# Expert weights addressed by two plain table numbers instead of one packed code

## What is computed

```python
qkv = rms_norm(x) @ w_qkv.T;  q, k, v = split(qkv)        # the mixer, on layernorm(x)
q, k = rms_norm(q), rms_norm(k)
w  = cumsum(exp(k), axis=1);  kv = cumsum(exp(k) * v, axis=1)
y  = sigmoid(q) * kv / (w + 1e-6)
u, g = split(y @ w_swiglu.T)
x = x + (layernorm(x) + (u * silu(g)) @ w_out.T)

flat = layernorm(x)                                        # the experts, 8 of them, 2 per token
topk = top_k(softmax(flat @ router_weight.T + router_bias), 2)
y = einsum('th,ehk->tek', flat, weight) + bias
x = x + flat + y[topk].sum(over the two)
```

## Time and profile before

| | |
|---|---|
| median of 3 runs | 1638.11 us (1636.93 to 1638.89) |
| the profiled execution, its own time | 1636.89 us |
| its span, first to last instruction | 1635.1 us |
| busy: PE, DVE, ACT, POOL | 1572.5, 1214.4, 570.6, 993.6 us |
| granted TensorE clock, mean | 0.993 |

### The profile page before, as it was taken

The page is one execution under the profiler, slowest core; times in us unless marked ns, Lnnn a source line. Parts: engine busy times, 40 slices in busy tenths (PEclk is TensorE's granted clock), DMA queues, the critical chain, the costliest instruction groups (busy, mean ns, idle before and its releaser), DMA issues.

```text
span 1635.1 us, 27374 instructions
## 1 busy us (share of the span) xinstructions
PE 1572.5 (96%) x7987; PEld 1284.8 (79%) x7987; DVE 1214.4 (74%) x2436; ACT 570.6 (35%) x1088; POOL 993.6 (61%) x1253
## 2 busy tenths in 40 slices
PE   8899999999999999999999999989999867899998
PEld 5788888888888888888888888778788755677786
DVE  7777778877877788778777877897887564565665
ACT  4333333333333333333333333323333222333433
POOL 2546666675577667765766586567663365565663
PEclk9999999999999999999999999999999989999999
DMA  6122333334333343333433343343425587599884
GB/s 234 49 93 91 128 134 126 122 127 147 117 117 117 117 142 127 135 123 132 152 117 117 117 143 116 117 143 117 143 98 188 175 269 227 161 368 372 317 312 178
DMA packets 135387, 258.57 MB, mean 158 GB/s; under 512 B 18519, under 2 KB 19297, under 8 KB 135242
## 3 DMA queue, kind: packets, MB, share of 16 engines
q1 hardware_dynamic: 118442, 222.62, 39.3%
q0 software_dynamic: 16800, 34.21, 6.3%
HBM read 321.00 MB, written 101.11 MB: 258 GB/s over the span
## 4 chain that ended last, share of the span: by engine, by line
PE 87%; DVE 3%; another core or an unknown queue 2%; SPq 2%; issue 2%; DMA 1%; ACT 1%; POOL 0%; POOLq 0%; DVEq 0%; ACTq 0%
PE pU L1348 4%; PE pG L1348 3%; PE pV L1348 3%; PE pG L1350 3%; PE pK L1348 3%; PE pO L1350 3%; PE pO L1348 3%; PE pO L1349 3%; PE pK L1350 3%; PE pG L1349 3%; PE pK L1349 3%; PE pV L1349 3%; PE pV L1350 3%; PE pQ L1348 3%; PE pQ L1349 3%; PE pQ L1350 3%
## 5 line engine op out<-in xcount | busy, mean ns | idle before, releaser
L784 DVE RECIPROCAL B<-B 128x512 f32<-128x512 f32 x64 | 214.6, 3353 | 2.2
L388 POOL TENSOR_SCALAR sa<-ss,hinv,ep 128x1 f32<-128x1 f32 x128 | 44.0, 344 | 238.7 <-ACT B L576 238.2
L402 POOL TENSOR_TENSOR F<-B,F 128x512 fp32r<-128x512 f32 x64 | 82.6, 1290 | 140.5 <-ACT F L598 140.5
L473 POOL DMA_INDIRECT out_dram<-B,tab x91 | 93.8, 1031 | 110.7 <-DVE B L866 66.0
L812 DVE SCALAR_TENSOR_TENSOR B<-B,nm,pO 128x512 f32<-128x512 f32 x64 | 47.8, 746 | 146.5 <-PE pO L1350 146.5
L433 POOL TENSOR_TENSOR R<-B,R 128x512 fp32r<-128x512 f32 x112 | 142.6, 1297 | 0.0
L428 POOL TENSOR_TENSOR B<-B 128x512 f32<-128x512 f32 x112 | 141.8, 1292 | 0.0
L1348 PE MATMUL pK<-R,F 128*128 128x512 f32 x256 | 106.3, 415 | 2.0 <-DVE F L744 2.0
L1348 PE MATMUL pG<-R,F 128*128 128x512 f32 x256 | 106.4, 416 | 1.5 <-POOL F L402 1.4
L1348 PE MATMUL pU<-R,F 128*128 128x512 f32 x256 | 106.3, 415 | 0.0
L1348 PE MATMUL pV<-R,F 128*128 128x512 f32 x256 | 101.4, 396 | 1.5 <-DVE B L758 1.5
(11 more groups left out here) (256 smaller groups left out, 4535.5 us busy)
## 6 DMA issues: line engine op xcount, KB each, us to landing
R<-pair_weights SPq DMA_DIRECT2D x93, 2048.0 KB, 11.7
pair_weights<-R SPq DMA_DIRECT2D x112, 512.0 KB, 3.9
B<-in_wm SPq DMA_DIRECT2D x112, 256.0 KB
B<-pair_biases SPq DMA_DIRECT2D x93, 256.0 KB, 12.4
x_scratch<-B SPq DMA_DIRECT2D x64, 264.0 KB
B<-in_x SPq DMA_DIRECT2D x64, 256.0 KB
B<-in_xt SPq DMA_DIRECT2D x32, 256.0 KB
XTB<-in_xt SPq DMA_DIRECT2D x32, 256.0 KB
```

The source lines that it names most:

```text
L388: p.tensor_scalar(sa[:, r, j:j + 1], ss[:, r, j:j + 1], hinv[:, 0:1], ep[:, r:r + 1], ALU.mult, ALU.add).then_inc(s[f"ra{j}"], 1)
L402: p.tensor_tensor(fr(3)[0], DD, fr(2)[1], ALU.subtract).then_inc(s["yl"], 1)
L473: p.indirect_dma_start(od, bass.IndirectOffsetOnAxis(ap=idx[:, J:J + 1], axis=0), YO[J % 4], None, bounds_check=T * 128 - 1, oob_is_err=Fa ...
L784: v.reciprocal(DD, DD).then_inc(s["rec"], 1)
```

## The change

The table holds plain numbers. `tw` now has slot x 4096, the column at which the slot begins in `R`; the bias block of slot s is now block s of `B`, so that its column is `tw >> 3`. `tc` has the number of the pair, and 64 is added (`SKIP`) where nothing is to be loaded: the address then lies outside of `pair_weights` and `pair_biases`, and the transfer is dropped (`bounds_check="skip_entire_dma"`). The tiles of the mixer that lay in `B`'s blocks 0 to 7 are renumbered, so that each shares its block with the same slot as before. The loads of the numbers no longer state limits (`min_val`, `max_val`).

```diff
+SKIP = 64.0
...
-        X = [blk(0), blk(1), blk(2)]
-        WT, KVT, EQT, DD = blk(4), blk(5), blk(6), blk(7)
-        XT = [blk(3), sb("XTB", [128, 512])[:, :]]
+        X = [blk(6), blk(7), blk(0)]
+        WT, KVT, EQT, DD = blk(2), blk(3), blk(4), blk(5)
+        XT = [blk(1), sb("XTB", [128, 512])[:, :]]
...
             def load_run(r):
                 slot = (6 + r) % 8
-                code = e.value_load(rc[0:1, r:r + 1], min_val=0, max_val=2 * NP - 1)
+                pair = e.value_load(rc[0:1, r:r + 1])
...
             def load_pair(t):
...
-                code = e.value_load(tc[0:1, t:t + 1], min_val=0, max_val=NP * 16 - 1)
-                slot, new, pair = code & 7, (code >> 3) & 1, code >> 4
-                e.dma_start(Rf[:, bass.ds(slot * 4096, 4096)],
+                pair, at = e.value_load(tc[0:1, t:t + 1]), e.value_load(tw[0:1, t:t + 1])
+                e.dma_start(Rf[:, bass.ds(at, 4096)],
                             pwd[bass.ds(pair, 1), :, :].rearrange("o p n -> p (o n)"),
-                            cond=new, max_dma_last_dim=2048).then_inc(dwb[(t - 2) % 8], 16)
+                            bounds_check="skip_entire_dma", max_dma_last_dim=2048).then_inc(dwb[(t - 2) % 8], 16)
...
-                e.dma_start(B[:, bass.ds(((slot + 2) & 7) * 512, 512)], pbd[bass.ds(pair, 1), :].broadcast_to([128, H]),
-                            cond=new).then_inc(dwb[(t - 2) % 8], 16)
+                e.dma_start(B[:, bass.ds(at >> 3, 512)], pbd[bass.ds(pair, 1), :].broadcast_to([128, H]),
+                            bounds_check="skip_entire_dma").then_inc(dwb[(t - 2) % 8], 16)
...
-                return ((v.value_load(tw[0:1, J:J + 1], min_val=0, max_val=7) + 2) & 7) * 512
+                return v.value_load(tw[0:1, J:J + 1]) >> 3
...
-                v.scalar_tensor_tensor(out=q4[:, 1, :], in0=qnum[:, :], scalar=16.0, in1=q4[:, 2, :],
-                                       op0=ALU.mult, op1=ALU.add).then_inc(s["rt"], 1)
+                v.tensor_scalar(q4[:, 2, :], c, 4096.0, None, ALU.mult)
+                v.tensor_scalar(q4[:, 1, :], qnum[:, :], SKIP, None, ALU.add).then_inc(s["rt"], 1)
...
-                at = pe.value_load(tw[0:1, J:J + 1], min_val=0, max_val=7) * 4096
+                at = pe.value_load(tw[0:1, J:J + 1])
```

More of the change, by code:

```diff
@@ L286, in load_run @@
                 slot = (6 + r) % 8
-                code = e.value_load(rc[0:1, r:r + 1], min_val=0, max_val=2 * NP - 1)
+                pair = e.value_load(rc[0:1, r:r + 1])
                 e.dma_start(Rf[:, slot * 4096:(slot + 1) * 4096],
[L289 to L292, removed]
+                            pwd[bass.ds(pair, 1), :, :].rearrange("o p n -> p (o n)"),
+                            bounds_check="skip_entire_dma", max_dma_last_dim=2048).then_inc(drun[r // 2], 16)
+                e.dma_start(blk(slot), pbd[bass.ds(pair, 1), :].broadcast_to([128, H]),
+                            bounds_check="skip_entire_dma").then_inc(drun[r // 2], 16)
             def load_pair(t):
@@ L954, in slots_of @@
                 ready()
-                v.scalar_tensor_tensor(out=q4[:, 2, :], in0=c, scalar=-8.0, in1=runq[:, :],
+                v.scalar_tensor_tensor(out=c, in0=c, scalar=-8.0, in1=runq[:, :],
                                        op0=ALU.mult, op1=ALU.add).then_inc(s["rt"], 1)
@@ L1074, in table @@
                     ready()
-                    v.scalar_tensor_tensor(out=ge, in0=qnum[:, :], scalar=0.5, in1=ge,
+                    v.scalar_tensor_tensor(out=ge, in0=qnum[:, :], scalar=-SKIP, in1=ge,
                                            op0=ALU.add, op1=ALU.mult).then_inc(s["rt"], 1)
@@ L1081, in table @@
                     ready()
-                    v.scalar_tensor_tensor(out=ge, in0=ge, scalar=2.0, in1=c,
-                                           op0=ALU.mult, op1=ALU.mult).then_inc(s["rt"], 1)
+                    v.tensor_tensor(ge, ge, c, ALU.mult).then_inc(s["rt"], 1)
                     yield
@@ L1113, in table @@
                 ready()
-                v.scalar_tensor_tensor(out=col, in0=c4[:, 3:4], scalar=8.0, in1=c4[:, 1:2],
+                v.scalar_tensor_tensor(out=col, in0=c4[:, 3:4], scalar=-SKIP, in1=c4[:, 1:2],
                                        op0=ALU.mult, op1=ALU.add).then_inc(s["rt"], 1)
@@ L1125, in table @@
                     ready()
-                    v.tensor_copy(rc[:, :], pX[0:1, 480:484]).then_inc(s["rt"], 1)
+                    v.tensor_scalar(rc[:, :], pX[0:1, 480:484], SKIP, None, ALU.add).then_inc(s["rt"], 1)
                 yield "table"
```

## The result

| | before | changed |
|---|---|---|
| median of 5 runs | 1638.11 us (1635.35 to 1638.89) | 1728.3 us (1727.57 to 1728.48) |
| span of the profiled execution | 1635.1 us | 1726.6 us |
| granted TensorE clock, mean | 0.993 | 0.992 |

The changed kernel takes 1.0547 times as long [1.0534, 1.0559]: 90 us more, where 72 were forecast, inside the range of 1690 to 1753.

What follows compares the result with a forecast made beforehand. TensorE's own pace, 3.21 us a tile, was taken as the bound, its sequencer running ahead at 1.9 us. A 4.3 us sequencer round adds 61 us in the second part and 11 in the first: 1710 us, range 1690 to 1753.

Steps and rivals of the forecast that it cites:

- TensorE's part, one k: TensorE's sequencer in the expert stage: three matmuls of one k take 415, 98 and 415 ns, 928 where TensorE needs 690.
- low end (151): Four-step test's added step free, 151 ns: 898 ns a k, round 4.2 us, +54, nothing in the first part, 1692 us.
- high end (190): Four-step test costs VectorE's 190 ns: 1036 ns a k, round 4.74 us, +90, with 25 in the first part, 1753 us.
- The round, 4.3 us: TensorE's sequencer needs 4.3 us a tile against TensorE's 3.21, so the sequencer becomes the bound.
- second part: Expert stage from the 25th tile to the 91st: 66 intervals at 4.3 us, 283.8 for 222.9 us, +61 us.
- its stalls of 11 us: Waits for weights and gathered rows in the second part, 11 us, counted as swallowed by the longer rounds.
- First part: Expert stage's first 24 tiles, 132 us: the longer sequencer round partly disappears in pauses, +11 us, ends 0 and 25.
- SyncE, VectorE, table: nothing: SyncE's pass 0.6 us shorter but hidden by the seven-tile lead; VectorE's later test and the table's changes cost nothing.
- The rhythm: Sign in the expert stage: matmuls start 0.1, 0.4, 0.4 us apart instead of 0.23.
- 1, slow only behind a load: TensorE's later tests cost 61 ns each, 718 ns a k, round 3.6 us, 1656 us; chance 0.08.
- 2, the sequencer stays ahead: Added sequencer instructions stay hidden at 3.21 us a round, waits for weights go, 1636 us; chance 0.05.
- 3, the clock falls too: TensorE's clock drops in half of the second part's tiles: +117 us, with 11 in the first, 1766 us; chance 0.06.

Runs made afterwards that it cites:

- e3: The changed kernel with the low weight blocks addressed by an untested register, the high blocks by one tested at each use: 1619.41 us, 1.0002 of before.
- e5: The changed kernel itself run again, on a chip where the kernel before takes 1641.69 us: 1727.49 us, 1.0519 of before.
- e1: The changed kernel with limits stated again where TensorE reads its number (0 to 28672): 1619.67 us, 1.0002 of before.
- e12: The same kernel as e1, compared on another chip: 1619.78 us, 1.0000 of before.
- e9: The changed kernel with limits stated but not tested on TensorE and VectorE, and TensorE's number read ahead of the transposes: 1633.86 us, 0.9946 of before.
- e2: The kernel before with no limits stated at TensorE's read of the slot number: 1716.24 us, 1.0594 of before.

## Why the prediction was right, and where its sizes were off

**What bounds the kernel.** Right: TensorE's pace of 3.21 us a tile with a sequencer that ran ahead, and 1.3 us a tile to spare. e3 puts four tests into that spare time and loses nothing.

**TensorE's part, one k.** Forecast 928 ns, measured 945. The test was put at 166 ns and is 173, the address at 31 and is 37; the gaps of 0.06 and 0.08 us read from one tile of the kernel before fit (232 less 173, 115 less 37). The tests' low end (151) and high end (190) held the value. (The high end's 1036 ns a k also has the 15 ns of the added step, which its sentence does not name; by 190 alone it is 1006.)

**The round, 4.3 us: the mis-sized term.** By the steps from start to start the smallest round is 4 x 945, less 23 for the shorter first test, plus 355 for the load, 106 for its wait and 126 for the wait of the transposes: 4.34 us. The shortest rounds in the second part are 4.40 us, a third of them are up to 4.46, and the mean is 300.3 / 66 = 4.55. The prediction took one undisturbed tile for all of them. What is added are now and then longer steps, but not longer tests. In the second part:

```profile
L1494 PEldq FUSED_REGOPS  x528: 37/96/173, 1417.0 to 1716.7; - x176
L1480 PEldq TENSOR_LOAD <-tab x66: 297/304/673, 1420.0 to 1715.9; - x66
```

From start to start, over 64 rounds, a round has 0.23 us beyond its shortest steps: 0.06 in the table load, 0.03 between the last wait and the first test, and 0.14 in gaps that are 0.03 to 0.19 us longer than usual behind single tests, asserts and addresses, whose own records stay at 173, 18 and up to 42 ns. The cause of these gaps is not seen in the trace. Before, such steps fell into the sequencer's 1.3 us to spare (one table load took 1000 ns there). Now each one is on the path. The 0.25 us between 4.3 and 4.55, times 66, are the 16 us by which the second part came out over the forecast (+77 for +61). That its stalls of 11 us are swallowed held: the second part ran at the sequencer's round, with no stall on top of it.

**First part.** +11 forecast, +11.6 measured, behind a first matmul 1.3 us later. This much agreement is luck in part, since only 12 of the 24 tiles were weighed. The 1.3 us themselves are no effect of the change: the same kernel began the stage at 1271.28 us in e5. Together 61 + 11 stood for 77.4 + 12.9 = 90.3; behind the last tile's first matmul another 1.2 us came.

**SyncE, VectorE, table: nothing.** Shown by e1 and e12, which keep all three, on chips where before takes 1619 us. On the slower kind e9 alone has no tests, with other edits beside, and its 7.8 us leave room for a small part of SyncE's. The pass of SyncE became 0.5 us shorter where 0.6 was forecast.

The forecast read SyncE's time from a single pass and left aside the 2% of the chain that the earlier trace rows put on SPq. The chain of the kernel before runs over SyncE and a bias transfer from 1438.79 to 1483.17 us (start, us, what):

```profile
1448.05 6.55 SPq L311
...
1469.74 13.30 DMA B<-pair_biases
```

There the DMA engines' share is 1.01 (1430 to 1510 us), a single transfer instruction holds SyncE for 6.55 us, and at the end TensorE waits 1.7 us: the lead of seven tiles has run out. Most of this time is in the transfer instructions and the transfers, which the change keeps. In the changed kernel the share in these 80 us is 0.79, and SPq and DMA are gone from the chain.

VectorE tests once a tile, as before, but now where the bias is read:

```profile
L857 DVEq FUSED_REGOPS  x182: 46/148/280, 1285.4 to 1717.2; - x182
```

Half of the 182 are tests of 250 to 280 ns, half addresses of 46; before, the test took 190.

**The rhythm** was put at 0.1, 0.4, 0.4 us and is 0.33, 0.24, 0.42. The reused block's matmul is handed on 0.1 us behind the first, but TensorE starts it only 0.33 us behind. The sum over a k was the sequencer's all the same.

**Rivals.** 1, slow only behind a load: refuted by the 173 ns of e2's tests. 2, the sequencer stays ahead: refuted by the result, though its reasoning is right below the threshold, as e3 shows. The Trainium skill ("Runtime: NRT & Kernel Launch", "Instruction fetch mechanics") names a floor of about 20 cycles an instruction. Taken as the price, it gives by estimate a round of 2.2 us, which is hidden; the trace lies far above that floor, with 77 ns from an assert of 18 ns to the next instruction, and 232 for a test. 3, the clock falls too: 1.00 granted in the second part; the swinging clock that "TensorE: Matmul & The Clock Gate" of the Trainium skill describes ("A second HAM failure mode: psum-queue depth-cycling") did not appear, though TensorE was fed for 3.21 of every 4.55 us.

## What to carry to other kernels

A register that addresses a tile should carry stated limits from its load on: without them each access is tested where it stands, and here one argument left out turned 10 sequencer instructions a tile into 28 and cost 5%. Before adding register work to an engine, set the sequencer's round (durations plus gaps of 0.06 to 0.08 us, from its own rows) beside the engine's: below the engine's pace it costs nothing, above it every tenth counts, so leave a margin for halts. And don't ask the busy share whether TensorE is fed; look at the distance between starts.

## What the runs showed beyond that

- The same kernel took 1618.99, 1619.36, 1638.11 and 1641.69 us on the chips used. In the traces the difference lies in the expert stage, three quarters of it in the first part (132.3 us against 118.3 in e1, and 222.9 against 218.2 in the second). The cause is not known from these runs. It is larger than most effects that one wants to measure, so a difference holds for its chip.
- A starved TensorE has a busy share of 97%, because a matmul that is handed on late has a longer record (493 ns for 396), at the same granted clock.
- The sequencer is uneven, but not in its tests: in the second part a test takes 173 ns at most, a table load 297 to 673, and single gaps are up to 0.19 us longer than usual. Records of register instructions up to 700 ns stand only in the first part.
